# Attention scores laid out with keys on the partitions and kept in SBUF until the maximum is known

## The chip, the cores and the metric

One NeuronCore of a Trainium2 chip runs the whole kernel. The metric is device time in microseconds (us). Engines are named as in the profile: PE (TensorE matmuls), PEld (its weight loads), DVE (VectorE), ACT (ScalarE), POOL (GpSimd), SP (SyncE, which issues the DMAs). PE writes only PSUM; ACT and DVE read PSUM; POOL works on SBUF.

## The reference, cut to what matters

```
x: (8, 2048, 256) f32;  W_qkv: (256, 768)
xn = layernorm(x)
q, k, v = split(xn @ W_qkv)
scores = q @ k.T / 16, causal mask (keys after the query are -inf)
attn = softmax(scores) @ v
out = x + attn + ffn(xn)          # ffn: a shared expert and one of 32 routed experts for each token
```

## The kernel before

Four stages run one after the other: `token_stage` (layer norm, shared expert, router), `routing_stage`, `expert_stage` (the routed experts), and `attention_stage`, the last one, which the change rewrites. Everything before about 1443 us of the profile is untouched.

Matrix products are made in three float32r passes of split operands, hi*hi, lo*hi, hi*lo (`split_matmuls`, L69 to L71). The weights of q and k are folded into one 256x256 matrix, so "queries" are x times that matrix and the keys are x itself.

In `attention_stage` there are 8 batches of 16 row blocks of 128 queries (B = 8, NB = 16). For each batch PE makes the queries (8 units of 512 columns), the values (8 units), and then for each row block i: the scores of its 128 queries (on partitions) against all (i+1)*128 keys, in up to four PSUM banks, with a bf16 matmul that adds the causal mask (L1243). DVE reduces them to the row maximum (L1101), ACT takes the exponential with its row sum (L1168), PE turns each 128x128 block so that keys come on partitions (L1255), ACT writes the high part of the turned block (L1177), DVE the low part (L1109), and PE weighs the values with them (136 blocks of a batch, three matmuls of 256 columns each). DVE scales the row by 1/sum and adds `base` (L1120).

POOL prepares `base` of each row block: `sum1` = routed + shared row (L1074), `base` = sum1 + x (L1076), then it copies the positions of the row block after next (L1058) and issues their gather (L1060). The program order on each engine is written out by hand. PE makes the scores of row i+1 between the transposes and the weighing of row i, so that DVE and ACT have that time for the softmax.

## Time and profile before

| | |
|---|---|
| time, median of 3 runs | 2554.9 us (2553.63, 2554.90, 2556.84) |
| span of the profiled execution, first to last instruction | 2553.1 us |
| busy: PE, PEld, DVE, ACT, POOL | 98%, 90%, 61%, 43%, 30% |
| attention stage in the profile | from 1443 us to the end |

A busy share is the time in which at least one instruction of the engine is under way. PE's matmuls overlap, so the cost of one in a dense stream is the distance from its start to the next start, which the timeline shows, and not its duration. The profile does not give the profiled execution's time apart from its span; the span is 0.5 us below the fastest of the three runs and 1.8 us below their median.

### The profile page before, as it was taken

How to read it: one execution, taken by the hardware profiler on the slowest of the kernel's cores; microseconds unless marked ns; L12 is line 12 of the kernel's file. 1: busy time of each engine (PE TensorE's matmuls, PEld its weight loads, DVE VectorE, ACT ScalarE, POOL GpSimd, SP SyncE). 2: the span in 40 equal slices, each digit the busy share in tenths (PEclk: the TensorE clock that was granted, in tenths of full speed). 3: DMA queues.
4: the chain of work that ended last, by engine and by line, in shares of the span. 5: the costliest groups of instructions: out<-in, count | busy, mean ns of one | idle time of the engine just before them, and what ended most of it. 6: DMA issues, size and time to landing. Idle time of an engine off the chain costs nothing. (4 is left out here: it accounts for less than half of the span.)

```text
span 2553.1 us, 51599 instructions
## 1 busy us (share of the span) xinstructions
PE 2491.2 (98%) x17497; PEld 2296.7 (90%) x17497; DVE 1565.0 (61%) x3433; ACT 1095.4 (43%) x1901; POOL 758.7 (30%) x920
## 2 busy tenths in 40 slices
PE   7999999998879999999999799999999999999999
PEld 5888888887779999999999799999999999999998
DVE  7777777775967777777777444544444444444453
ACT  3333333333646655566555333333333333333332
POOL 1111111110034444444444342423232322323141
PEclk9999999999889999999999899999999999999999
DMA  4434434342367777777777732322323232323230
GB/s 141 149 128 139 143 133 141 136 139 101 135 224 237 237 231 238 236 240 236 233 234 239 226 110 71 116 82 84 113 67 120 73 114 63 110 79 110 67 94 19
DMA packets 264190, 369.37 MB, mean 145 GB/s; under 512 B 17424, under 2 KB 186896, under 8 KB 264080
## 3 DMA queue, kind: packets, MB, share of 16 engines
q1 hardware_dynamic: 250064, 329.60, 38.3%
q0 software_dynamic: 14016, 38.29, 6.0%
q8 instruction: 71, 1.16, 0.2%
q14 instruction: 39, 0.32, 0.0%
HBM read 254.57 MB, written 113.25 MB: 144 GB/s over the span
## 5 line engine op out<-in xcount | busy, mean ns | idle before, releaser
L69 PE MATMUL t_psO<-t_v_hi,t_pT_hi 128*128 128x256 f32 x1088 | 316.1, 291 | 0.5 <-DVE t_pT_lo L1109 0.5
L71 PE MATMUL t_psO<-t_v_lo,t_pT_hi 128*128 128x256 f32 x1088 | 307.5, 283 | 0.0
L70 PE MATMUL t_psO<-t_v_hi,t_pT_lo 128*128 128x256 f32 x1088 | 307.2, 282 | 0.0
L1101 DVE TENSOR_REDUCE t_negmax<-t_psS 128x1 f32<-128x128 f32 (+15 forms) x128 | 165.1, 1290 | 217.0 <-PE t_psS L1243 216.7
L1168 ACT ACTIVATE t_prob<-t_psS,t_negmax 128x128 f32<-128x128 f32 (+15 forms) x128 | 149.9, 1171 | 337.0 <-DVE t_negmax L1101 335.8
L832 DVE TENSOR_TENSOR e_wlo<-e_raw,e_whi 128x1024 fp32r<-128x1024 f32 x162 | 198.1, 1223 | 152.2 <-ACT e_whi L875 152.2
L1074 POOL TENSOR_TENSOR t_sum<-t_routed,t_shr 128x256 f32<-128x256 f32 x128 | 94.2, 736 | 639.6 <-DVE t_outb L1120 624.9
L808 POOL DMA_INDIRECT e_xg<-xs_rows,e_slot x164 | 248.5, 1515 | 97.0 <-POOL e_slot L804 63.2
L1177 ACT CAST t_pT_hi<-t_psT 128x512 fp32r<-128x512 f32 (+2 forms) x320 | 152.0, 530 | 281.2 <-PE t_psT L1255 281.2
L69 PE MATMUL t_psS<-t_x_hi,t_q_hi 128*128 128x512 f32 (+2 forms) x640 | 243.4, 380 | 0.0
L71 PE MATMUL t_psS<-t_x_lo,t_q_hi 128*128 128x512 f32 (+2 forms) x640 | 233.0, 364 | 0.0
L70 PE MATMUL t_psS<-t_x_hi,t_q_lo 128*128 128x512 f32 (+2 forms) x640 | 232.4, 363 | 0.0
L1109 DVE TENSOR_TENSOR t_pT_lo<-t_psT,t_pT_hi 128x512 fp32r<-128x512 f32 (+2 forms) x320 | 180.3, 606 | 63.4 <-ACT t_pT_hi L1177 63.1
L69 PEld LDWEIGHTS t_psO<-t_v_hi,t_pT_hi 128*128 128x128 f32 x1088 | 208.5, 192 | 1.1 <-DVE t_pT_lo L1109 0.8
L70 PEld LDWEIGHTS t_psO<-t_v_hi,t_pT_lo 128*128 128x128 f32 x1088 | 208.1, 191 | 0.3
L71 PEld LDWEIGHTS t_psO<-t_v_lo,t_pT_hi 128*128 128x128 f32 x1088 | 207.9, 191 | 0.0
L69 PE MATMUL e_psD<-e_whi,e_h_hi 128*128 128x256 f32 x640 | 187.1, 292 | 4.3 <-issue 4.3
L69 PE MATMUL e_psG<-e_x_hi,e_whi 128*128 128x256 f32 x640 | 180.0, 281 | 3.6 <-DVE e_x_lo L840 3.6
L70 PE MATMUL e_psD<-e_whi,e_h_lo 128*128 128x256 f32 x640 | 180.7, 282 | 0.0
L71 PE MATMUL e_psD<-e_wlo,e_h_hi 128*128 128x256 f32 x640 | 180.3, 282 | 0.0
L71 PE MATMUL e_psU<-e_x_lo,e_whi 128*128 128x256 f32 x640 | 180.0, 281 | 0.0
L69 PE MATMUL e_psU<-e_x_hi,e_whi 128*128 128x256 f32 x640 | 179.7, 281 | 0.0
(190 smaller groups left out, 7287.2 us busy)
## 6 DMA issues: line engine op xcount, KB each, us to landing
e_raw<-in_L_ffn_routed_gate_w SPq DMA_DIRECT2D x83, 512.0 KB
e_raw<-in_L_ffn_routed_up_w SPq DMA_DIRECT2D x83, 512.0 KB
e_raw<-in_L_ffn_routed_down_w SPq DMA_DIRECT2D x82, 512.0 KB
routed_rows<-e_dout SPq DMA_DIRECT2D x80, 256.0 KB
a_xt<-in_L_attn_x SPq DMA_DIRECT2D x32, 512.0 KB, 4.5
xT_high<-a_xT_hi SPq DMA_DIRECT2D x32, 512.0 KB, 3.7
xT_low<-a_xT_lo SPq DMA_DIRECT2D x32, 512.0 KB, 3.9
xs_rows<-a_xs SPq DMA_DIRECT2D x32, 512.0 KB, 3.0
```

Source lines behind the costliest of these rows:

```text
L69: nc.tensor.matmul(out, hi, rhi, start=first, stop=False, skip_group_check=True)
L70: nc.tensor.matmul(out, lo, rhi, start=False, stop=False, skip_group_check=True)
L71: return nc.tensor.matmul(out, hi, rlo, start=False, stop=last, skip_group_check=True)
L808: g.indirect_dma_start(out=xg[:, k, h], out_offset=None, in_=xs, in_offset=bass.IndirectOffsetOnAxis(slot[:, k, h:h + 1], 0)).then_inc(x_i ...
L832: v.tensor_tensor(wlo[k][:, n], raw[k][:, n], whi[k][:, n].bitcast(F32), ALU.subtract).then_inc(wlo_ok, 1)
L1074: g.tensor_tensor(sum1[:, k], routed[:, k], shr[:, kg, j], ALU.add).then_inc(sum_ok, 1)
L1101: v.tensor_reduce(negmax[:, i % 2:i % 2 + 1], psS[:].rearrange("p a n -> p (a n)")[:, 0:(i + 1) * P], AX.X, ALU.max, negate=True).then_inc ...
L1109: v.tensor_tensor(pT_lo[s][:, 0:m], psT[:, (before[i] + q) % 3, 0:m], pT_hi[s][:, 0:m].bitcast(F32), ALU.subtract).then_inc(pl_ok, 1)
L1168: s.activation(prob[i % 2][:, 0:(i + 1) * P], psS[:].rearrange("p a n -> p (a n)")[:, 0:(i + 1) * P], ACT.Exp, bias=negmax[:, i % 2:i % 2 ...
L1177: s.copy(pT_hi[t][:, 0:m], psT[:, (before[i] + q) % 3, 0:m]).then_inc(ph_ok, 1)
```

## The change

Only `attention_stage` changes. Scores come with 128 keys on the partitions and up to 512 queries (a group of four row blocks) in the free dimension, so nothing has to be turned before the values are weighed. A tile (b, G, j) is key block j for query group G: 4(G+1) tiles in a group, the last four on the diagonal and cut to 512, 384, 256, 128 columns; 40 tiles in a batch, 320 in all. The order of a batch is G = 0, 1, 2, 3, with 4, 8, 12, 16 tiles.

Because the maximum of a query is now over partitions and over tiles, ACT copies each score tile to SBUF (`keep_score`, a ring of 21 slots) and DVE folds it into a running maximum over tiles (`highest`). After a group, PE turns this [128, 512] tile (`turn`, four transposes), DVE reduces it and spreads it on a diagonal (`row_max`), one matmul with ones brings it to all partitions (`broadcast`), and ACT stores it (`keep_shift`). POOL adds this shift to every stored score tile, in place (`lower`). ACT then takes the exponential twice, once as f32 and once rounded as the high part (`exps`), DVE makes the low part (`p_low`), and PE weighs the values 21 steps after the scores (`weigh`), into four PSUM banks, one for each row block of the group; a column of ones beside the values gives the row sum.

All engines walk through one list of steps; a step is one score tile, and engines differ in how many steps they lag. POOL's work on the rows (`sum1`, `base`, `gather`) is the same as before; it now shares the queue with `lower`. Score PSUM is three banks.

The diff, cut to its core (the old lines are those of the listing above; PE's `queries`, `values` and the loads change in indices only):

```diff
+class Plan:
+    LAG = 21
+    BANKS = 3
...
+        self.tiles = [(b, G, j) for b in range(B) for G in range(GB) for j in range(J * (G + 1))]
...
+            q_step.setdefault(max(0, self.first[g] - 3), []).append(g)
+                v_step.setdefault(self.first[g] + 10 + u, []).append((g, u))
...
+    XR, VR, QR, PR, HR = 5, 5, 2, 3, 3
+    W = D + 2
+    plan = Plan(B, NB, GB)
+    LAG, BANKS, T = plan.LAG, plan.BANKS, plan.T
+    SR = LAG
...
+            def load_rows(n):
+                k, g, h = n % 2, n // 2, n % 2
+                wait(sp, base_ok, 2 * (n - 1))
+                sp.dma_start(xr[:, k], x_g[g][:, 2 * h:2 * h + 2]).then_inc(r_in[k], 16)
+                sp.dma_start(shr[:, k], sh_g[g][:, 2 * h:2 * h + 2]).then_inc(r_in[k], 16)
...
+            def gather(r):
+                k = r % 2
                 wait(pool, sum_ok, r - 1)
+                wait_apart(pool, d_in[k], 16 * (r // 2), passed)
+                g_.tensor_copy(pos[:, k], keep.position[:, r:r + 1]).then_inc(pos_ok, 1)
                 wait_apart(pool, pos_ok, r + 1, passed)
+                g_.indirect_dma_start(out=routed[:, k], out_offset=None, in_=d_rows,
+                                      in_offset=bass.IndirectOffsetOnAxis(pos[:, k, 0:1], 0)).then_inc(d_in[k], 16)
+            def add_up(r):
+                k, n = r % 2, r // 2
+                wait(pool, r_in[n % 2], 32 * (n // 2 + 1))
+                wait(pool, d_in[k], 16 * (r // 2 + 1))
+                g_.tensor_tensor(sum1[:, k], routed[:, k], shr[:, n % 2, r % 2], ALU.add).then_inc(sum_ok, 1)
+                wait(pool, sum_ok, r + 1)
+                wait(pool, o_ok, r - 1)
+                g_.tensor_tensor(base[:, k], sum1[:, k], xr[:, n % 2, r % 2], ALU.add).then_inc(base_ok, 1)
+                if r + 2 < R:
+                    gather(r + 2)
+            def lower(t):
+                g, c0 = plan.group(t), plan.cut(t) * P
+                wait(pool, shift_ok, g + 1)
+                wait(pool, u_act, plan.s_unit[t] + 1)
+                s = score[:, t % SR, c0:]
+                g_.tensor_tensor(s, s, shift[:, g % HR, c0:], ALU.add).then_inc(sub_ok, 1)
+            g_.memset(ones[:].bitcast(F32), 1.0).then_inc(ones_ok, 1)
+            g_.memset(v_hi[:, :, :, D:D + 1].bitcast(F32), 1.0).then_inc(ones_ok, 1)
+            g_.memset(v_hi[:, :, :, D + 1:W].bitcast(F32), 0.0).then_inc(ones_ok, 1)
+            gather(0)
+            gather(1)
+            for step in range(T + LAG + 2):
+                t = step - LAG + 4
+                if 0 <= t < T:
+                    lower(t)
+                if 0 <= step - LAG + 2 < T:
+                    for r, _ in plan.rows_done(step - LAG + 2):
+                        add_up(r)
...
+            def highest(t):
+                g, c0 = plan.group(t), plan.cut(t) * P
+                _, G, j = plan.tiles[t]
+                m, s = top[:, g % 2, c0:], score[:, t % SR, c0:]
+                if j == 0 and G > 0:
+                    return
+                wait(dve, u_act, plan.s_unit[t] + 1)
+                if j < 2:
+                    wait(dve, top_mm, g - 1)
+                if G == 0 and j == 0:
+                    v.tensor_copy(m, s).then_inc(top_ok, 1)
+                elif G > 0 and j == 1:
+                    v.tensor_tensor(m, score[:, (t - 1) % SR, c0:], s, ALU.max).then_inc(top_ok, 1)
+                else:
+                    wait(dve, top_ok, plan.tops[t - 1])
+                    v.tensor_tensor(m, m, s, ALU.max).then_inc(top_ok, 1)
+            def row_max(g):
+                wait(dve, top_mm, g + 1)
+                v.tensor_reduce(negmax[:], psX[:].rearrange("p (a n) -> p a n", a=J), AX.X, ALU.max,
+                                negate=True).then_inc(max_ok, 1)
+                wait(dve, max_ok, g + 1)
+                wait(dve, shift_mm, g)
+                v.tensor_tensor(spread[:], keep.ident[:].unsqueeze(1).to_broadcast([P, J, P]),
+                                negmax[:].unsqueeze(2).to_broadcast([P, J, P]), ALU.mult).then_inc(spread_ok, 1)
+            def p_low(t):
+                c0 = plan.cut(t) * P
+                wait(dve, exp_ok, t + 1)
+                wait(dve, pv_mm, t - PR + 1)
+                v.tensor_tensor(p_lo[:, t % PR, c0:], prob[:, t % 2, c0:], p_hi[:, t % PR, c0:].bitcast(F32),
+                                ALU.subtract).then_inc(lo_ok, 1)
+            def output(t, r, a):
+                k = r % 2
+                wait(dve, pv_mm, t + 1)
+                v.reciprocal(rinv[:, k:k + 1], psO[:, a, D:D + 1]).then_inc(rinv_ok, 1)
                 wait(dve, rinv_ok, r + 1)
                 wait(dve, base_ok, r + 1)
+                wait(dve, o_out[k], 16 * (r // 2))
+                v.scalar_tensor_tensor(out=outb[:, k], in0=psO[:, a, 0:D], scalar=rinv[:, k:k + 1], in1=base[:, k],
                                        op0=ALU.mult, op1=ALU.add).then_inc(o_ok, 1)
+            for step in range(T + LAG + 2):
+                for g in plan.q_step.get(step, ()):
+                    for c in range(C):
+                        q_low(g, c)
+                if step < T:
+                    for g, u in plan.v_step.get(step, ()):
+                        v_low(g, u)
+                    highest(step)
+                for g in plan.ended_at(step - 1):
+                    row_max(g)
+                if 0 <= step - LAG + 1 < T:
+                    p_low(step - LAG + 1)
+                if 0 <= step - LAG - 1 < T:
+                    for r, a in plan.rows_done(step - LAG - 1):
+                        output(step - LAG - 1, r, a)
...
+            def keep_score(t):
+                n, c0 = plan.s_unit[t], plan.cut(t) * P
+                wait(act, exp_ok, t - SR + 1)
+                wait(act, u_mm, n + 1)
+                s.copy(score[:, t % SR, c0:], psS[:, n % BANKS, c0:]).then_inc(u_act, 1)
+            def keep_shift(g):
+                if g >= HR:
+                    wait(act, sub_ok, plan.last[g - HR] + 1)
+                wait(act, shift_mm, g + 1)
+                s.copy(shift[:, g % HR], psX[:]).then_inc(shift_ok, 1)
+            def exps(t):
+                c0 = plan.cut(t) * P
+                wait(act, sub_ok, t + 1)
+                wait(act, lo_ok, t - 1)
+                s.activation(prob[:, t % 2, c0:], score[:, t % SR, c0:], ACT.Exp)
+                wait(act, pv_mm, t - PR + 1)
+                s.activation(p_hi[:, t % PR, c0:], score[:, t % SR, c0:], ACT.Exp).then_inc(exp_ok, 1)
+            for step in range(T + LAG + 2):
+                for g in plan.q_step.get(step, ()):
+                    for c in range(C):
+                        q_high(g, c)
+                if step < T:
+                    for g, u in plan.v_step.get(step, ()):
+                        v_high(g, u)
+                    keep_score(step)
+                for g in plan.ended_at(step - 2):
+                    keep_shift(g)
+                if 0 <= step - LAG + 2 < T:
+                    exps(step - LAG + 2)
...
+            def free_bank(n):
+                if n - BANKS in plan.splits:
+                    wait(pe, split_ok, plan.splits[n - BANKS])
+                else:
+                    wait(pe, u_act, n - BANKS + 1)
...
+            def scores(t):
+                n, g, c0 = plan.s_unit[t], plan.group(t), plan.cut(t) * P
+                b, G, j = plan.tiles[t]
+                k, q = (b * GB + j // J) % XR, g % QR
+                diagonal = j >= J * G
+                cols = slice((j % J) * P, (j % J + 1) * P)
+                wait(pe, split_ok, plan.splits[plan.q_unit[g, C - 1]])
+                free_bank(n)
+                for d in range(C):
+                    mm = split_matmuls(nc, psS[:, n % BANKS, c0:], x_hi[:, k, d, cols], x_lo[:, k, d, cols],
+                                       q_hi[:, q, d, c0:], q_lo[:, q, d, c0:], d == 0, d == C - 1 and not diagonal)
+                if diagonal:
+                    mm = nc.tensor.matmul(psS[:, n % BANKS, c0:c0 + P], keep.mask_bf[:], keep.ident_bf[:],
+                                          start=False, stop=True, skip_group_check=True)
+                mm.then_inc(u_mm, 1)
+            def turn(g):
+                wait(pe, top_ok, plan.tops[plan.last[g]])
+                wait(pe, shift_ok, g)
+                for a in range(J):
+                    mm = nc.tensor.transpose(psX[:, a * P:(a + 1) * P], top[:, g % 2, a * P:(a + 1) * P], keep.ident[:])
+                mm.then_inc(top_mm, 1)
+            def broadcast(g):
+                if g == 0:
+                    pe.wait_ge(ones_ok, 3)
+                wait(pe, spread_ok, g + 1)
+                nc.tensor.matmul(psX[:], ones[:], spread[:].rearrange("p a n -> p (a n)"),
+                                 start=True, stop=True).then_inc(shift_mm, 1)
+            def weigh(t):
+                b, G, j = plan.tiles[t]
+                g, kv, kp = b * GB + G, (b * GB + j // J) % VR, t % PR
+                wait(pe, split_ok, plan.splits[plan.v_unit[b * GB + j // J, (j % J) // 2]])
+                wait(pe, lo_ok, t + 1)
+                for a in range(plan.cut(t), J):
+                    cols = slice(a * P, (a + 1) * P)
+                    last = j == J * G + a
+                    if j == 0:
+                        wait(pe, o_ok, (g - 1) * J + a + 1)
+                    nc.tensor.matmul(psO[:, a, 0:W], p_hi[:, kp, cols], v_hi[:, kv, j % J], start=j == 0, stop=False,
+                                     skip_group_check=True)
+                    nc.tensor.matmul(psO[:, a, 0:W], p_lo[:, kp, cols], v_hi[:, kv, j % J], start=False, stop=False,
+                                     skip_group_check=True)
+                    mm = nc.tensor.matmul(psO[:, a, 0:D], p_hi[:, kp, cols], v_lo[:, kv, j % J, 0:D], start=False, stop=last,
+                                          skip_group_check=True)
                 mm.then_inc(pv_mm, 1)
+            for step in range(T + LAG):
+                for g in plan.q_step.get(step, ()):
+                    for c in range(C):
+                        queries(g, c)
+                if step < T:
+                    for g, u in plan.v_step.get(step, ()):
+                        values(g, u)
+                    scores(step)
+                for g in plan.ended_at(step - 1):
+                    turn(g)
+                for g in plan.ended_at(step - 2):
+                    broadcast(g)
+                if 0 <= step - LAG < T:
+                    weigh(step - LAG)
```

## Rows read from the trace of the kernel before

**Rows 1.** The page, busy time of each engine over the span.
```profile
PE 2491.2 (98%) x17497; PEld 2296.7 (90%) x17497; DVE 1565.0 (61%) x3433; ACT 1095.4 (43%) x1901; POOL 758.7 (30%) x920
```
**Rows 2.** Busy time by stretch: PE, PEld, DVE, ACT, POOL, clock, DMA.
```profile
1718.00:1855.00 137.00, 137.00 (x944) 125.47 (x943) 62.47 (x104) 47.93 (x88) 41.54 (x64) 1.00 0.29 93
1855.00:1992.00 137.00, 137.00 (x944) 125.51 (x944) 62.48 (x104) 47.95 (x88) 41.55 (x64) 1.00 0.29 93
```
**Rows 3.** The chain that ended last, from 1440 us to the end, by line.
```profile
by line: PE t_psS L69 17.5%; PE t_psS L71 17.0%; PE t_psS L70 17.0%; PE t_psO L69 12.0%; PE t_psO L71 11.6%; PE t_psO L70 11.6%; PE t_psT L1255 10.9%; PE t_psS L1243 0.8%; DMA t_x_lo<-xT_low 0.5%; issue 0.3%; ACT L1168 0.1%; DVE t_pT_lo L11
```
**Rows 4.** Timeline of PE (start, duration, instruction).
```profile
2300.55 0.60 PE L1255 MATMUL t_psT<-keep_ident,t_prob 128*128 128x128 f32 x4
2300.91 0.48 PE L69 MATMUL t_psS<-t_x_hi,t_q_hi 128*128 128x512 f32 x1
2301.22 0.39 PE L70 MATMUL t_psS<-t_x_hi,t_q_lo 128*128 128x512 f32 x1
...
2302.38 0.28 PE L69 MATMUL t_psS<-t_x_hi,t_q_hi 128*128 128x256 f32 x1
...
2303.09 0.23 PE L1243 MATMUL t_psS<-keep_mask_bf,keep_ident_bf 128*128 128x128 bf16 x1
2303.12 0.37 PE L69 MATMUL t_psS<-keep_v_hi,t_x_hi 128*128 128x256 f32 x1
2303.33 0.28 PE L70 MATMUL t_psS<-keep_v_hi,t_x_lo 128*128 128x256 f32 x1
...
2306.07 0.71 PE L1255 MATMUL t_psT<-keep_ident,t_prob 128*128 128x128 f32 x5
2306.53 0.47 PE L69 MATMUL t_psS<-t_x_hi,t_q_hi 128*128 128x512 f32 x1
```
**Rows 5.** Groups by shape, ACT and DVE, from 1480 us (busy, mean ns).
```profile
L1177 ACT CAST t_pT_hi<-t_psT 128x512 fp32r<-128x512 f32 x223 | 120.2, 593 | 127.8 <-PE t_psT L1255 127.8
L1109 DVE TENSOR_TENSOR t_pT_lo<-t_psT,t_pT_hi 128x512 fp32r<-128x512 f32 x223 | 143.7, 687 | 62.9 <-ACT t_pT_hi L1177 62.9
L1120 DVE SCALAR_TENSOR_TENSOR t_outb<-t_psO,t_rinv,t_base 128x256 f32<-128x256 f32 x125 | 60.5, 484 | 162.8 <-issue 159.4 <-DVE t_rinv L1115 1.5
L1115 DVE RECIPROCAL t_rinv<-t_rowsum 128x1 f32<-128x1 f32 x125 | 19.2, 154 | 0.0
```
**Rows 6.** Timeline of POOL in the attention stage, one row block.
```profile
2301.76 0.74 POOL L1074 TENSOR_TENSOR t_sum<-t_routed,t_shr 128x256 f32<-128x256 f32 x1 [0.22 <-DVE t_outb L1120]
2302.58 0.74 POOL L1076 TENSOR_TENSOR t_base<-t_sum,t_xr 128x256 f32<-128x256 f32 x1
2303.27 0.18 POOL L1058 COPY t_pos<-keep_position 128x1 int32<-128x1 int32 x1
2304.27 0.99 POOL L1060 DMA_INDIRECT t_routed<-routed_rows,t_pos  x1 [0.82 <-POOL t_pos L1058]
```
**Rows 7.** Timeline of POOL and DVE in the routing stage, 638 to 650 us.
```profile
638.90 4.43 DVE L632 TENSOR_TENSOR r_moved<-ranks_one_hot,r_shift 128x4096 f32<-128x4096 f32 x1
...
640.30 4.15 POOL L583 TENSOR_TENSOR keep_v_lo<-r_wqkv,keep_v_hi 128x512 fp32r<-128x512 f32 x1 [3.73 <-ACT keep_v_hi L591]
...
647.83 1.39 POOL L585 TENSOR_TENSOR keep_a_lo<-r_a,keep_a_hi 128x512 fp32r<-128x512 f32 x1 [3.38 <-ACT keep_a_hi L597]
...
648.14 1.17 DVE L635 CAST r_pos_i<-r_pos 128x128 int32<-128x128 f32 x1
...
649.91 0.22 DVE L640 CAST r_token<-r_token_i 128x128 f32<-128x128 int32 x1
```
**Rows 8.** Timeline of POOL and DVE in the expert stage, 1199 to 1207 us.
```profile
1201.63 1.23 DVE L832 TENSOR_TENSOR e_wlo<-e_raw,e_whi 128x1024 fp32r<-128x1024 f32 x1 [2.01 <-ACT e_whi L875]
...
1201.95 1.76 POOL L808 DMA_INDIRECT e_xg<-xs_rows,e_slot  x1 [0.81 <-POOL e_slot L804]
...
1205.16 0.96 POOL L808 DMA_INDIRECT e_xg<-xs_rows,e_slot  x1 [1.45 <-issue]
```
**Rows 9.** Busy time by stretch in the routing stage (columns as in rows 2).
```profile
640.00:650.00 10.00, 5.36 (x16) 3.71 (x14) 9.83 (x8) 2.45 (x4) 5.54 (x2) 0.67 1.03 354
```

More of the change, by code:

```diff
@@ L960, in attention_stage @@
     J = GT // P
-    QU = C * GB
-    VU = NB // 2
-    groups = [i // 4 + 1 for i in range(NB)]
-    before = [sum(groups[:i]) for i in range(NB + 1)]
-    TG = before[NB]
-    assert TG % 4 == 0 and NB % 2 == 0 and C * GB % 4 == 0
+    XR, VR, QR, PR, HR = 5, 5, 2, 3, 3
[3 more added lines that the diff above has]
+    SR = LAG
+    NGR, R = plan.NGR, B * NB
     with ExitStack() as st:
@@ new lines, in store @@
+            def store(r):
+                wait(sp, o_ok, r + 1)
+                sp.dma_start(out_g[r // J][:, r % J], outb[:, r % 2]).then_inc(o_out[r % 2], 16)
+            for g in range(XR):
+                load_x(g)
+                if g < 2:
+                    load_rows(g)
+            for step in range(T + LAG + 2):
+                for g in range(XR, NGR):
+                    if plan.first[g] - 12 == step:
+                        load_x(g)
+                if 0 <= step - LAG - 1 < T:
+                    for r, _ in plan.rows_done(step - LAG - 1):
+                        store(r)
+                        if r % 2 == 1 and r // 2 + 2 < R // 2:
+                            load_rows(r // 2 + 2)
@@ L1116, in output @@
                 wait(dve, rinv_ok, r + 1)
-                wait(dve, pv_mm, b * TG + before[i + 1])
                 wait(dve, base_ok, r + 1)
-                wait(dve, o_out[k], 16 * half)
-                v.scalar_tensor_tensor(out=outb[:, k], in0=psO[:, k], scalar=rinv[:, k:k + 1], in1=base[:, k],
+                wait(dve, o_out[k], 16 * (r // 2))
+                v.scalar_tensor_tensor(out=outb[:, k], in0=psO[:, a, 0:D], scalar=rinv[:, k:k + 1], in1=base[:, k],
                                        op0=ALU.mult, op1=ALU.add).then_inc(o_ok, 1)
-            for u in range(QU):
-                q_low(0, u)
@@ L1201, in _, with q_high, v_high @@
-            each_pair(act, B // 2, pair)
+            def q_high(g, c):
+                n = plan.q_unit[g, c]
+                wait(act, u_mm, n + 1)
+                if g >= QR:
+                    wait(act, u_mm, plan.s_unit[plan.last[g - QR]] + 1)
+                s.copy(q_hi[:, g % QR, c], psS[:, n % BANKS]).then_inc(u_act, 1)
+            def v_high(g, u):
+                n = plan.v_unit[g, u]
+                wait(act, u_mm, n + 1)
+                if g >= VR:
+                    wait(act, pv_mm, plan.last_pv(g - VR) + 1)
+                s.copy(v_hi[:, g % VR, 2 * u:2 * u + 2, 0:D],
+                       psS[:, n % BANKS].rearrange("p (a d) -> p a d", a=2)).then_inc(u_act, 1)
@@ L1247, in transposes @@
-            def transposes(b, i, q):
-                n = b * TG + before[i] + q
-                s = (before[i] + q) % 3
-                if q == 0:
-                    wait(pe, exp_ok, b * NB + i + 1)
-                if before[i] + q >= 3:
-                    wait(pe, pl_ok, n - 2)
-                for m in range(4 * q, min(4 * q + 4, i + 1)):
-                    mm = nc.tensor.transpose(psT[:, s, m % 4], prob[i % 2][:, m * P:(m + 1) * P], keep.ident[:])
-                mm.then_inc(t_mm, 1)
```

345 lines of the change are left out of this document (108 added, 237 removed).

## The prediction

> **What bounds the kernel now.** I read the page first, then the busy time by stretch, the chain that ended last, the timelines, and the groups by shape. PE is busy 98% of the span [rows 1]. In the attention stage each batch takes 137.3 us with PE busy all of it, at full clock, and DVE, ACT and POOL less than half [rows 2]. The chain there is PE's from end to end: scores, queries and values 51%, weighing 35%, transposes 10.9% [rows 3]. So work taken off PE there shortens the time one for one, until another engine can't follow.
>
> **PE's prices** are start distances [rows 4]. A 512-column pass costs 0.232 us, from 2301.22 to 2302.38 for five; a 256-column pass 0.118, from 2302.38 to 2303.09 for six. Four transposes take 0.36 before the next matmul and lengthen that one by 0.08 (2300.91 to 2301.22 instead of 0.232): 0.09 each and 0.08 for each run of them. A mask matmul costs 0.12 in the same way.
>
> **What leaves PE, for a batch.** 136 transposes in 40 runs: 136*0.09 + 40*0.08 = 15.4 us, near the chain's 10.9% of 137. Score passes: off the diagonal both kernels have 24 pieces of 512 columns. On it the old kernel has widths 256, 256, 384, 512 in each group, the new one 512, 384, 256, 128: 24 passes go from 256 to 128 columns. No float32r pass of 128 columns is in this trace. Its floor is a transpose's 0.09, its ceiling a 512-column pass; I take the floor, gain 24*0.03 = 0.7, and keep 24*0.14 = 3.4 us loss as the other end. Queries, values, mask and weighing stay in count (408 passes of 256 columns; two more columns are 1/128 of that). **What comes:** four runs of four transposes, 1.8, and four 512-column passes, 1.0. Net 15.4 + 0.7 - 2.8 = 13.3 us saved, 124.0 of PE work in a batch, 107 us in the stage.
>
> **What ACT and DVE get.** ACT: a 512-column copy is 0.59 [rows 5], and a tile needs three such passes, 1.8 us, where a step of PE is on average 124/40 = 3.1. DVE: two 512-column operations a tile at 0.69 [rows 5], 1.4 us, and the four maxima, low parts and outputs. Neither is a bound by itself. POOL is.
>
> **POOL's new load.** A row block costs 0.82 (sum to base) + 0.69 (base to copy) + 1.00 (copy to gather) + 0.99 (gather), 3.5 us, 3.7 with what lies before the next operation [rows 6]. `lower` is a two-input operation of 512 columns, which takes 1.39 us when nothing is in its way [rows 7], with its handoff 1.5; the cut tiles at 2.9 ns a column (0.74 for 256 [rows 6]) 1.15, 0.8 and 0.45. A batch is 24*1.5 + 4*3.9 + 16*3.7 = 111 us, against PE's 124: 41.5 before [rows 2], when it waited for the rest.
>
> **Where it can't hide.** Each diagonal tile carries a row block, and the four diagonal tiles of G = 3 are followed at once by the four of the next batch's G = 0: eight in a row. A cycle of POOL there is 3.7 + a lower, 4.2 to 5.2 us. It can't be done ahead: `base` of row r waits for `output` of r-2, which DVE makes only after the next score tile is made and copied (1.4 + 0.6), `highest` and `p_low` (0.7 each) and its own 0.15 + 0.48 [rows 5], with handoffs 4.3 us behind the weighing. Behind that `base` in POOL's queue stand the gather and the `lower` of the tile three further on; for that wait ACT's exponentials, behind them ACT's next `keep_score`, which frees PE's banks, and DVE's `p_low`, for which PE's `weigh` waits.
>
> Number the tiles from the first diagonal one of G = 3 as 0, and set the clock to zero at its output, 4.3 us after its weighing. PE's next ten steps are, by its prices: ten score tiles 12.5 us (those 21 further on), two query units 2.8, two value units 2.8, `turn` and `broadcast` 0.8, weighings 10.0, together 28.8: alone it would end tile 10 at 24.5. On POOL the first wait is of tile 2's `base`, at zero; `lower` of tile 10 ends after 4.85 + 4.5 + 4.15 + 5.2 + 5.2 + 4.4 = 28.3. Two exponentials and a low part with handoffs (2.6 to 3) and 1.4 of weighing end tile 10 at 32.7: PE stands still 8 us. From there POOL has four lowers (5.0), a sum and three more cycles (15.3) to the `base` of tile 15, the last row of G = 1, at 48.7. Its output, some 2.3 later, is what the fourth block of tile 16 waits for, since that block overwrites its PSUM bank: 51.4 where PE would be at 47.4, 4 us more. After G = 2's four, `lower` of G = 3's first tile needs a shift that is ready only then (at S); two rows are queued behind it, and the second output comes at S + 4.8, so `lower` two tiles on ends at S + 14.4, its weighing at S + 18.5, where PE alone has S + 14.7: 4 us. 16 us a batch.
>
> **The lock.** A POOL operation that reads two operands ran 4.15 us instead of 1.39 for the same shape [rows 7]. It began at 640.30 while DVE worked on two SBUF inputs until 643.33, and ended 1.1 us after that. The other way round, a DVE cast of 128 columns, 0.22 elsewhere, took 1.17 us and ended with POOL's operation of 647.83 to 649.22. A gather took 1.76 us under such a DVE operation and 0.96 without [rows 8]. So one excludes the other for its whole length. In the old stage DVE's large operations have an operand in PSUM, and POOL's adds are a steady 0.74. In the new one `highest`, `p_low` and the spreading read two SBUF operands, and so does POOL. In a batch they hold the inputs about 50 us (77 tile operations of 0.29 to 0.69, four spreads) beside POOL's 75. In a cycle of the cluster DVE has 1.2 us of it. About 0.7 falls on POOL's adds and lowers, not on its 2 us around the gather, and a gather met by it loses 0.2: I take 0.9 a cycle (ends: 0, and all 1.2 with a wait on both sides, 1.8). The first cluster has five cycles before `lower` of tile 10 and a low part that is held too: its stall goes from 8 to 13.5. The second has four lowers and three cycles more, and waits for a `p_low` ahead of its output: 4 to 10.5. The third has two cycles: 4 to 6. 30 us a batch.
>
> The Trainium skill, "SBUF — State Buffer", section "Who interferes with whom", has this as a rule: a DVE instruction with two SBUF inputs contends with a GpSimd instruction that reads SBUF, and the later one blocks fully. By that rule, and the trace agrees, the sum is the one below; without it, it would be that of the second rival.
>
> **The sum.** Seven boundaries between batches at 24, the first batch's G = 0 and 1 at 12, eight third clusters at 6, and the end, where PE has no score tiles left to make between the weighings while POOL needs 50 us for 16 tiles and six rows: 20 more. 168 + 12 + 48 + 20 = 248, less 107: +141. 2553.1 + 141 = 2694 in the profiled execution, and with the 1.8 us to the median 2696. SP moves the same bytes beside a DMA share of 0.29 [rows 2]; its row loads now wait for every second output, 5 us ahead of their use, and cost nothing while POOL is late anyhow. The chain `turn`, `row_max`, `broadcast` (DVE 0.69 + 0.69 between two PE steps) holds PE where both steps are short, twice a batch by some 0.6 us; that falls into the same waits, and I count none of it.
>
> **Rivals.**
> POOL and the lock bound the stage, my forecast: 2696, own range 2630 to 2780 by the two ends of the lock and the narrow pass. Chance 0.50.
> The lock costs almost nothing, because DVE's operations fall beside the gather; the row cycles alone: 7*12 + 6 + 8*4 + 15 = 137, less 107, +30: 2585, between 2565 and 2630. For it: DVE is free half the time. Against it: 125 us of exclusive use in a batch where PE has 124 us of work. Chance 0.14.
> The other side, faster: POOL's row work doesn't hold `weigh`. Then PE waits only at each group's start, where its fourth block needs `output` of the row before, about 2 us, 64 us in the stage, with 10 at the end: 107 - 74 = 33, 2522. It decides at one point: a row cycle of POOL of at most 3.2 us, where `lower` of tile 10 comes at 20.4 instead of 28.3. For it: the 21 steps of distance. Against: 3.5 us are in the rows before any `lower`. Chance 0.18.
> Worse: PE, standing still again and again, gets its low clock. At 640 us, with PE busy half of a stretch, the granted clock was 0.67, between its two levels of 2.4 and 1.2 GHz [rows 9]. Half speed in the some 35 us of work of the clusters costs another 15 to 25 us a batch where it isn't hidden by POOL: 2820 to 2900. Chance 0.18.
>
> **The numbers.** A measurement of this kernel can tell some 0.2% from no change. The range goes from 2565 to 2880: it takes the first two and most of the last, and leaves out the faster case and the far end. Faster 0.17, same 0.03, slower 0.80.
>
> **What would show it.** In the profile after: L1255 gone but for 128 transposes; PE busy about 80% of the attention stage; a batch at 150 to 158 us; POOL over 80% busy there and first in the chain; idle time of PE before `weigh` put down to `p_low` or to `output`; `lower` of 512 columns with a minimum near 1.4 us and a mean of 1.8 to 2.1, DVE's `p_low` with the same scatter. I am wrong if `lower` is never longer than 1.5 us, if POOL waits for most of its time, or if PE's idle time lies at the groups' starts alone.

## The result and the profile after

| | before | after |
|---|---|---|
| median of 4 runs | 2554.98 us | 2780.18 us (2779.45 to 2783.1) |
| ratio | | 1.0882, 95% interval 1.0865 to 1.0898 |
| profiled span | 2553.1 us | 2781.3 us |

The change makes the kernel 8.8% slower: on the side that was forecast, 84 us above its point of 2696, inside the whole range (2565 to 2880), and just above the 2630 to 2780 that the forecast case had for itself. The page of the changed kernel, busy time of each engine:

```profile
PE 2493.6 (90%) x16569; PEld 2260.6 (81%) x16569; DVE 1872.3 (67%) x3665; ACT 1269.1 (46%) x2317; POOL 1197.2 (43%) x1243
```

PE was 98% busy [rows 1] and is 90% busy. Its busy sum has hardly moved although transposes are gone: at the low clock a pass takes nearly twice as long. The busy time by stretch says so (columns as in [rows 2]):

```profile
1600.00:1760.00 160.00, 133.73 (x815) 117.86 (x814) 99.84 (x133) 67.40 (x136) 92.47 (x101) 0.91 0.23 73
2240.00:2400.00 160.00, 129.46 (x798) 114.40 (x797) 96.65 (x129) 67.26 (x137) 93.74 (x104) 0.91 0.25 80
```

A batch takes about 165 us where it took 137 [rows 2]. PE stands for about 30 of them and has a mean granted clock of 0.91, where it had 1.00. POOL is busy for only 58% of them. The groups of POOL and DVE by shape (busy, mean ns, idle before):

```profile
L1145 POOL TENSOR_TENSOR t_score<-t_score,t_shift 128x512 f32<-128x512 f32 x224 | 282.7, 1286 | 149.1 <-ACT t_shift L1264 147.5
L1136 POOL TENSOR_TENSOR t_base<-t_sum,t_xr 128x256 f32<-128x256 f32 x128 | 117.4, 917 | 308.2 <-DVE t_outb L1216 300.2
...
L1191 DVE TENSOR_TENSOR t_top<-t_top,t_score 128x512 f32<-128x512 f32 x168 | 268.8, 1600 | 237.5 <-ACT t_score L1258 237.3
```

`lower` takes 1.29 us, less than the 1.39 of [rows 7], so POOL isn't held by DVE in it. Its other operations do pay something: `sum1` takes 0.97 us in the mean where it took 0.74, `base` 0.92 for 0.74, the copy of positions 0.40 for 0.18, the gather 1.03 for 0.99, together 0.67 us a row. The large change is on the other side. It is DVE's `highest` that has a mean of 1.60 us where two-input operations of that width took 0.69 [rows 5]. The two DVE lines one by one (least, median, largest duration in ns):

```profile
L1191 DVE TENSOR_TENSOR t_top<-t_top,t_score x264: 279/693/12762, 1459.6 to 2725.8; 128x512 f32<-128x512 f32 x84, 128x384 f32<-128x384 f32 x16, 128x128 f32<-128x128 f32 x16, 128x256 f32<-128x256 f32 x16
L1206 DVE TENSOR_TENSOR t_p_lo<-t_prob,t_p_hi x320: 276/684/13177, 1496.4 to 2775.6; 128x512 fp32r<-128x512 f32 x128, 128x256 fp32r<-128x256 f32 x32
```

The median is undisturbed, the largest is 12.8 and 13.2 us: 17 operations of 512 columns last over 3 us, 145 us together. The timeline of POOL, of DVE and of PE around one of them:

```profile
2251.70 0.99 POOL L1126 DMA_INDIRECT t_routed<-routed_rows,t_pos  x1 [0.81 <-POOL t_pos L1124]
2252.72 15.64 POOL L1145 TENSOR_TENSOR t_score<-t_score,t_shift 128x512 f32<-128x512 f32 x13
2268.32 1.17 POOL L1133 TENSOR_TENSOR t_sum<-t_routed,t_shr 128x256 f32<-128x256 f32 x1
```
```profile
2255.71 12.08 DVE L1191 TENSOR_TENSOR t_top<-t_top,t_score 128x512 f32<-128x512 f32 x1 [3.65 <-ACT t_score L1258]
2267.70 1.21 DVE L1206 TENSOR_TENSOR t_p_lo<-t_prob,t_p_hi 128x512 fp32r<-128x512 f32 x1
```
```profile
2256.53 0.39 PE L71 MATMUL t_psS<-t_q_lo,t_x_hi 128*128 128x512 f32 x1
2269.06 0.55 PE L1355 MATMUL t_psO<-t_v_hi,t_p_hi 128*128 128x258 f32 x1 [12.14 <-DVE t_p_lo L1206]
2269.41 0.42 PE L1357 MATMUL t_psO<-t_v_hi,t_p_lo 128*128 128x258 f32 x1
2269.62 0.41 PE L1359 MATMUL t_psO<-t_v_lo,t_p_hi 128*128 128x256 f32 x1
```

POOL makes a gather and then 13 shifts without a gap, 1.20 us each. DVE begins one `highest` in the middle of that run and ends it 12.08 us later, 0.5 us before the run does. `p_low` is behind it in DVE's queue, PE's weighing waits for that, and when PE goes on its passes stand 0.21 us apart instead of 0.118 [rows 4]: the low clock. This happens once a batch, in G = 3's run. A smaller one, 4 to 7 us, comes in G = 2's shorter run.

**Where the time went.** From PE's records in the attention stage I took the time between one's end and the next one's start, and the stretches with a granted clock under 0.75. In those PE was busy 177 of 262 us; I counted half of the 177 as lost, and the rest as work at full clock. The passes' own distances give a little less: 0.214 us for 0.118, and 0.427 for 0.232, are a loss of 45%, some 80 us instead of 89. The split is good to some 10 us in another way too: *noshift*, *gap* and *early* (below) make the same matmuls and read 1016, 1028 and 1028 us of work.

| us in the stage | before | after | predicted for after |
|---|---|---|---|
| work at full clock | 1099 | 1014 (-85) | -107 |
| PE idle | 1 | 227 | +248 |
| lost to the low clock | 1 | 89 | none in the sum; a rival |
| the stage | 1101 | 1330 | |

The idle time ahead of the weighings, by the tile weighed, sorts into the prediction's clusters (us a batch): the first (G = 0 and 1) 7.8, the second (G = 2) 5.7, the third (G = 3) 13.7. The prediction had 13.5, 10.5 and 6. The sum is about right and its places are not. By single tiles, 93 of the 227 us stand ahead of tile 26 (the third of G = 3), the one that the long `highest` holds up. Another 66 stand ahead of the fourth block of the groups' first tiles (0, 4, 12, 24 of a batch), where PE waits for `output`. Ahead of tile 6, the prediction's tile 10, it is 0.6 us a batch, where the prediction had the 8 us of its first cluster. PE at those places in one batch (tile 0's fourth block, tile 4's fourth block, tile 6's first):

```profile
2323.15 0.39 PE L1355 MATMUL t_psO<-t_v_hi,t_p_hi 128*128 128x258 f32 x1 [2.86 <-DVE t_outb L1216]
...
2339.09 0.58 PE L1355 MATMUL t_psO<-t_v_hi,t_p_hi 128*128 128x258 f32 x1 [3.80 <-DVE t_outb L1216]
...
2346.56 0.28 PE L1355 MATMUL t_psO<-t_v_hi,t_p_hi 128*128 128x258 f32 x1
```

### The profile page after: what moved, and what is told of

Read it like the earlier page. It is cut to its first block and busy times, and to the rows that moved or that the text cites. A ratio compares the mean times of both kernels' runs of the same rounds, so it can differ in the third digit from the quotient of the medians.

```text
span 2781.3 us, 52329 instructions
## 1 busy us (share of the span) xinstructions
PE 2493.6 (90%) x16569; PEld 2260.6 (81%) x16569; DVE 1872.3 (67%) x3665; ACT 1269.1 (46%) x2317; POOL 1197.2 (43%) x1243
## 5 line engine op out<-in xcount | busy, mean ns | idle before, releaser
L1355 PE MATMUL t_psO<-t_v_hi,t_p_hi 128*128 128x258 f32 x1088 | 344.9, 317 | 217.1 <-DVE t_p_lo L1206 125.1
L1191 DVE TENSOR_TENSOR t_top<-t_top,t_score 128x512 f32<-128x512 f32 (+3 forms) x264 | 317.6, 1203 | 275.0 <-ACT t_score L1258 274.6
L1355 PEld LDWEIGHTS t_psO<-t_v_hi,t_p_hi 128*128 128x128 f32 x1088 | 222.7, 205 | 252.6 <-issue 174.0
L1145 POOL TENSOR_TENSOR t_score<-t_score,t_shift 128x512 f32<-128x512 f32 (+1 forms) x320 | 358.0, 1140 | 150.1 <-ACT t_shift L1264 147.5
L1357 PE MATMUL t_psO<-t_v_hi,t_p_lo 128*128 128x258 f32 x1088 | 322.8, 297 | 0.0
L1359 PE MATMUL t_psO<-t_v_lo,t_p_hi 128*128 128x256 f32 x1088 | 321.7, 296 | 0.0
L1206 DVE TENSOR_TENSOR t_p_lo<-t_prob,t_p_hi 128x512 fp32r<-128x512 f32 (+1 forms) x320 | 289.0, 904 | 17.5 <-ACT t_p_hi L1272 17.4
L69 PE MATMUL t_psS<-t_q_hi,t_x_hi 128*128 128x512 f32 (+3 forms) x640 | 246.7, 385 | 1.4 <-DVE t_q_lo L1167 1.4
L70 PE MATMUL t_psS<-t_q_hi,t_x_lo 128*128 128x512 f32 (+3 forms) x640 | 245.6, 384 | 0.0
L71 PE MATMUL t_psS<-t_q_lo,t_x_hi 128*128 128x512 f32 (+3 forms) x640 | 244.3, 382 | 0.0
```

The costliest lines, as they stand in the source:

```text
L69: nc.tensor.matmul(out, hi, rhi, start=first, stop=False, skip_group_check=True)
L70: nc.tensor.matmul(out, lo, rhi, start=False, stop=False, skip_group_check=True)
L71: return nc.tensor.matmul(out, hi, rlo, start=False, stop=last, skip_group_check=True)
L1145: g_.tensor_tensor(s, s, shift[:, g % HR, c0:], ALU.add).then_inc(sub_ok, 1)
L1191: v.tensor_tensor(m, m, s, ALU.max).then_inc(top_ok, 1)
L1206: v.tensor_tensor(p_lo[:, t % PR, c0:], prob[:, t % 2, c0:], p_hi[:, t % PR, c0:].bitcast(F32), ALU.subtract).then_inc(lo_ok, 1)
```

## The experiments

All ratios are to the kernel before in the same session (medians 2555.3 to 2556.3 us), with their 95% interval. Theory A: POOL's shifts follow each other so closely that a DVE operation with two SBUF inputs is shut out of a whole run of them. Theory B, the prediction's: the row cycle of POOL with a small toll for each contact. Theory C: DVE's in-order queue is the bound.

**gap.** `lower` waits until the shift before it is finished:

```
+                wait(pool, sub_ok, t)
                 s = score[:, t % SR, c0:]
```

> Each of POOL's shifts (lower) waits until the one before it has finished, which leaves a gap of under 0.1 us between two of them. Theory A (a run of POOL's shifts without a gap keeps a DVE operation with two SBUF inputs out until the whole run is over): DVE's longest highest or p_low falls from 13 us to under 2.5 us, PE's idle time before weigh put down to p_low falls from 125 us to under 50, and the time falls by 60 to 110 us, to 2670 to 2720 us. Theory B (the loss is POOL's row cycle in the runs of diagonal tiles, as in the prediction): the gap costs POOL 320 times 0.08 us, the time stays within 2770 to 2800 us.

Measured: 2676.71 us, ratio 1.0482 (1.0464 to 1.0499), 103 us faster than the changed kernel though a wait is added. The largest `highest`, in the view of that line:

```profile
L1192 DVE TENSOR_TENSOR t_top<-t_top,t_score x264: 281/696/2552, 1458.4 to 2623.0; 128x512 f32<-128x512 f32 x84, 128x384 f32<-128x384 f32 x16, 128x128 f32<-128x128 f32 x16, 128x256 f32<-128x256 f32 x16
```

12.8 us has become 2.6 (and `p_low`'s 13.2 has become 2.9); theory A had asked for less than 2.5. PE's wait for `p_low` has gone from 125 to 41 us. PE idles 139 us and loses 57 to the low clock. So theory A holds for 103 us. The clusters are now 6.8, 4.1 and 4.9 us a batch, near the 8, 4 and 4 that the prediction had before it added the lock, but not for its reason: 54 of the 139 us are waits for `output` at the groups' starts, and ahead of tile 6 there are still only 0.6 us a batch.

**noshift.** The shift is left out: POOL only counts, and the exponentials take the unshifted scores scaled by 0.001. The kernel then lacks the subtraction of the maximum, though it still finds, turns and spreads it.

```
-                g_.tensor_tensor(s, s, shift[:, g % HR, c0:], ALU.add).then_inc(sub_ok, 1)
+                pool.sem_inc(sub_ok, 1)
```

> Leaves the shift out of the computation: POOL only counts the semaphore on, and the exponentials take a scale of 0.001 so that their arguments stay small. POOL has the row work alone. Theory A: 2520 to 2570 us, PE waits mainly at the starts of the groups for output. Theory B: the cycle of 3.7 us a row still holds the runs of eight diagonal tiles, 3 to 6 us of standing a batch: 2560 to 2610 us.

Measured: 2553.08 us, ratio 0.9991 (0.9982 to 1.0001). PE's waits in the whole kernel, longest sums (us, times, longest):

```profile
PE t_psO L1354 <- DVE t_outb L1215: 40.7, 31, 2.9
PE t_psO L1354 <- issue: 17.9, 21, 1.4
```

Some 59 us at the groups' starts, where the faster rival had 64; 41 of them are the wait of the fourth block for `output`. The time is that of theory A (2520 to 2570). The work saved pays just for the idle time and the low clock (67 idle and 19 lost). So without the shift the two kernels are level, and the 225 us between them come with it.

**nogather, onegather, sync1.** What opens the run to DVE? In *nogather* all gathers but the first two are left out, with their copies of positions, so later rows take stale routed values. *onegather* keeps of them only the one of each group's last row. *sync1* is the changed kernel with one completion wait, at the second shift after each gather:

```
+                if plan.rows_done(t - 4) and t >= 4:
+                    wait(pool, sub_ok, t)
```

> Leaves out all gathers of routed rows but the first two, and their position copies; the two adds of a row stay. A row costs POOL 1.6 us instead of 3.7. Theory A: POOL runs further ahead and the long waits of DVE stay, the time falls only by the part of the row cycle: 2690 to 2750 us. Theory B: POOL keeps up with PE everywhere: 2540 to 2600 us.

> As the run without gathers (which leaves the routed rows out), but with the one gather of each group that stands right before the run of shifts off the diagonal. Theory A2: the long waits of DVE come back, with DVE operations of 5 to 13 us in the runs of G = 2 and 3, and the time rises from 2649 by 50 to 100 us, to 2700 to 2750 us, though POOL has only 2 us a group more to do. Theory A1 gives no reason for a change: 2645 to 2670 us, no DVE operation over 2 us.

> As the changed kernel, but the second shift after each gather waits until all before it have finished; within a run of 4 to 13 shifts no further wait stands. Theory A1 (any run of POOL operations without a gap keeps DVE out): one gap lets one DVE operation in, the rest of the run still keeps the next one out for 5 to 10 us; the time stays above 2730 us. Theory A2 (the gather leaves POOL's parts out of step, and only then does a run without a gap keep DVE out; one wait for completion brings them in step again, and from then on DVE gets its turn after each shift): DVE's longest operation falls under 3 us and the time is that of the run with a gap before every shift, 2660 to 2690 us.

| | us | ratio (interval) |
|---|---|---|
| nogather | 2649.43 | 1.0369 (1.0352 to 1.0386) |
| onegather | 2794.49 | 1.0934 (1.0915 to 1.0952) |
| sync1 | 2668.75 | 1.0444 (1.0426 to 1.0461) |

*nogather* came out under theory A's range and above B's, so both were wrong as they stood. Its longest DVE operation is 1.9 us, although POOL's runs have no gap in them:

```profile
2034.71 15.97 POOL L1143 TENSOR_TENSOR t_score<-t_score,t_shift 128x512 f32<-128x512 f32 x11
```
```profile
2041.91 1.68 DVE L1189 TENSOR_TENSOR t_top<-t_top,t_score 128x512 f32<-128x512 f32 x1 [4.34 <-ACT t_score L1256]
2043.51 1.77 DVE L1204 TENSOR_TENSOR t_p_lo<-t_prob,t_p_hi 128x512 fp32r<-128x512 f32 x1
```

So a run without a gap is not enough to shut DVE out. That is why A was split into A1 (any such run does it) and A2 (only one behind a gather does). *onegather* and *sync1* both speak for A2; *onegather* goes beyond its 2700 to 2750 us and its 13 us for one operation. *nogather* also bears on theory B: `lower` of the prediction's tile 10 ends 20.2 to 22.1 us behind the first output, near the 20.4 at which the prediction's faster rival was to come true with 2522 us. The time is 2649, and PE waits 70.6 us for `output`.

The timeline of *onegather*, POOL and DVE:

```profile
2093.63 0.99 POOL L1126 DMA_INDIRECT t_routed<-routed_rows,t_pos  x1 [0.81 <-ACT t_score L1258]
2094.64 15.07 POOL L1145 TENSOR_TENSOR t_score<-t_score,t_shift 128x512 f32<-128x512 f32 x13
```
```profile
2094.53 16.42 DVE L1206 TENSOR_TENSOR t_p_lo<-t_prob,t_p_hi 128x512 fp32r<-128x512 f32 x1
2110.87 0.15 DVE L1212 RECIPROCAL t_rinv<-t_psO 128x1 f32<-128x1 f32 x1
```

One gather ahead of the run, with its copy of positions, is enough: `p_low` takes 16.42 us. It began 0.11 us before the run did, while the gather was still under way, and still lost. And of *sync1* in the same kind of run:

```profile
2037.44 17.18 POOL L1147 TENSOR_TENSOR t_score<-t_score,t_shift 128x512 f32<-128x512 f32 x12 [0.17 <-POOL t_score L1147]
```
```profile
2040.04 1.71 DVE L1193 TENSOR_TENSOR t_top<-t_top,t_score 128x512 f32<-128x512 f32 x1 [4.34 <-ACT t_score L1260]
2041.67 1.77 DVE L1208 TENSOR_TENSOR t_p_lo<-t_prob,t_p_hi 128x512 fp32r<-128x512 f32 x1
2044.01 1.13 DVE L1193 TENSOR_TENSOR t_top<-t_top,t_score 128x512 f32<-128x512 f32 x1 [0.57 <-ACT t_score L1260]
```

After one wait of 0.17 us the engines take turns: POOL's shift goes from 1.20 to 1.43 us in the mean (17.18 for 12), DVE's operations take 1.1 to 1.8. The gather's own 1 us isn't the cost (*nogather* gains only 19 us over *sync1*). What it leaves behind is, and one completion wait clears it. No run parts the gather from the copy of positions just ahead of it.

**dve.** DVE makes all the shifts, at `step - LAG + 3`, between its `p_low` and `output`:

```
+                if 0 <= step - LAG + 3 < T:
+                    lower(step - LAG + 3)
```

> DVE makes the shift, one step ahead of the exponentials; POOL has the row work alone. DVE's load of a batch goes from 75 to about 100 us, under PE's 124. Theory A: no run of POOL is left, DVE's operations stay under 1.5 us: 2540 to 2620 us. Theory B: about the same from POOL, but a theory C, DVE's in-order queue becomes the bound with three operations of 0.69 us a tile behind each other, would give 2640 us or more.

Measured: 2659.60 us, 1.0414 (1.0396 to 1.0431). No `highest` or `p_low` lasts over 1.5 us (the longest shift is 1.7), as theory A asked, yet the time isn't A's 2540 to 2620, and only 17 us under *gap*. PE waits 91.7 us, 55 times, for `output`, which stands behind three operations of DVE's step, and 1.6 us for `p_low`. That is theory C: DVE's queue.

**early, rows.** *early* is *gap* with `output` moved from the end of DVE's step to its start. *rows* is *early* with the gather reading `keep.position` itself, without POOL's copy and the wait for it.

> The gap before every shift, and DVE's output moved from the end of its step to the start, before highest and p_low. The fourth block of each group's first tile waits for it: 54 us of PE's idle time in the run with the gap, 41 without any shift. I expect 20 to 50 us less than 2677: 2627 to 2657 us. If POOL's row cycle alone sets the time there, POOL gets its release earlier too, but no more than that.

> As the run before, and the gather takes its positions from the kept table itself, without the copy and the wait for it: POOL's row goes from 3.7 to about 2.0 to 2.5 us. If the row cycle in the runs of diagonal tiles carries most of the 124 us between the runs with and without the shift, the time falls by another 40 to 80 us, to 2560 to 2600 us; if the lock between POOL and DVE carries it, by less than 25 us.

*early* 2618.63 us, 1.0246 (1.0229 to 1.0263): 58 us off *gap*, more than the 20 to 50 expected. So the place of `output` in DVE's step was worth that much. PE's longest waits in it:

```profile
PE t_psO L1356 <- DVE t_p_lo L1207: 73.0, 73, 2.9
PE t_psO L1356 <- issue: 31.2, 22, 2.1
```

Its wait for `output`, 54.4 us in *gap*, has nearly gone (2.1), while the one for `p_low` has grown from 40.9. *rows* 2624.03 us, 1.0267 (1.025 to 1.0284), where 2560 to 2600 was expected if the row cycle carried most of what was left. POOL's row cycle did get shorter: `lower` of the prediction's tile 10 ends 24.4 to 26.2 us behind the first output, 27.8 to 31.4 in *early*. The time didn't fall. So the length of the row cycle is not what holds this kernel.

**warm.** The changed kernel with 75 matmuls of ones that nobody reads, where PE waits longest, to keep it busy:

```
+                if G == 3 and j == 2:
+                    wait(pe, shift_ok, min(g + 2, NGR))
+                    for _ in range(75):
+                        nc.tensor.matmul(psX[:, 0:P], ones[:], ones[:], start=True, stop=True)
```

> The changed kernel, with 75 extra matmuls of 128 columns (ones by ones, into a bank that is free then, read by nobody) that TensorE runs at tile 26 of each batch, just before it waits for that tile's p_low. At 0.11 us a pass they take about 8 us, and TensorE idles 11.6 us there a batch in the changed kernel (92.6 us over 8 batches), so they should lie inside the idle time. Theory (the idle time brings the clock down, and the passes that follow run at half speed: 89 us of the 2780 by my reading of the trace, most of it behind this wait): the granted clock stays up, the batches get 3 to 8 us shorter, 2715 to 2755 us. Rival (the low clock follows from something else, or its passes run inside later waits anyway): 2775 to 2790 us, with the granted clock up or not. A second rival, the extra matmuls come to lie on the path where the wait is short: over 2790.

Measured: 2782.57 us, 1.0882 (1.0864 to 1.09): no gain. PE's timeline in the same batch as above:

```profile
2257.73 8.49 PE L1352 MATMUL t_psX<-t_ones 128*128 128x128 f32 x75
...
2271.40 0.58 PE L1359 MATMUL t_psO<-t_v_hi,t_p_hi 128*128 128x258 f32 x1 [5.18 <-DVE t_p_lo L1206]
```

The matmuls lay inside the wait as meant, but PE idles 5.18 us more behind them, and its first pass then still takes 0.58. By my count the low clock costs 76 instead of 89 us, while waits at other tiles grew by 9. The little clock won was used up by waiting. The time is the first rival's. The run speaks against counting all 89 us as time that a full clock would give back, but it touched only 13 of them, and their true worth stays open.

**lag24, split24, behind24.** *lag24* is *early* with `LAG` 24 instead of 21. *split24* is *lag24* with the shifts of odd tiles on DVE, each engine counting in a semaphore of its own. *behind24* gives DVE only those tiles whose shift would stand right behind a row's sums on POOL:

```
+        behind = [t >= 3 and bool(plan.rows_done(t - 3)) for t in range(T)]
```

> The kernel 'early' (a completion wait ahead of every shift, output moved to the start of DVE's step; 2618.6 us) with the distance between a tile's scores and its weighing raised from 21 to 24 steps. The tiles whose rows run on POOL between shifts then have three more steps (some 8 us) between the shift's arrival for the last group of a batch and its use. Theory (what is left is the late shifts in the rows' clusters, a latency): TensorE's waits at tiles 26 and 4 fall, 2580 to 2605 us. Rival (what is left is contention that lengthens DVE's p_low at every tile, a throughput): no gain, 2612 to 2630 us.

> As lag24, with the shifts of odd tiles made by DVE (three steps' distance before the tile is weighed plus one more) and those of even tiles by POOL. POOL then has half the shifts between its row sums, DVE some 76 more of 0.5 to 0.7 us (about 6 us a batch more than lag24, DVE then near 75% busy). Theory (POOL's shifts in the clusters of row sums, and the lock that they take with DVE, make the time that is left): 2550 to 2590 us, near the kernel before. Rival (DVE's in-order queue becomes the bound, as when it made all the shifts: 2659.6 us): 2600 to 2640 us.

> As split24 (2559.5 us), but DVE makes just the 16 shifts of a batch that would stand right behind a row's sums on POOL (tiles 3 to 6, 11 to 14, 23 to 26, 39 and the next 0 to 2), and POOL the 24 others. In split24 the time that is left stands mostly ahead of tiles 4, 6, 12, 14 and 24, whose shifts POOL makes behind row sums (8.3, 8.5, 5.0, 11.5 and, for tile 4, 12.6 + 7.3 us of TensorE's idle 87). Theory (POOL's late shifts are what is left): those waits go, some 30 to 45 us off, 2515 to 2540 us, faster than both kernels. Rival (DVE now has four shifts together with its outputs and is the late one there): 2555 to 2590 us, with TensorE still waiting for p_low at the same tiles.

| | us | ratio (interval) | PE idle | lost to clock |
|---|---|---|---|---|
| early | 2618.63 | 1.0246 (1.0229 to 1.0263) | 114 | 28 |
| lag24 | 2597.11 | 1.0159 (1.0142 to 1.0175) | 102 | 21 |
| split24 | 2559.52 | 1.0013 (1.0004 to 1.0023) | 79 | 14 |
| behind24 | 2577.02 | 1.0097 (1.007 to 1.0123) | 79 | 17 |

Busy time of *split24* in one stretch:

```profile
1600.00:1760.00 160.00, 150.64 (x982) 133.84 (x982) 114.62 (x174) 82.86 (x164) 84.73 (x91) 1.00 0.26 81
```

PE at full clock and 94% busy. *lag24* and *split24* came out in the ranges of their theories. *lag24* is not clean evidence for its own: PE's idle time ahead of tile 26 fell from 20 to 3 us, but ahead of tile 4 it rose from 16 to 21. *split24* takes back 221 of the 225 us and is no faster than the kernel before. *behind24* was to be faster than both and is a miss; the rival's time came. Its PE waits 23.6 us for `p_low`, where *split24*'s waits 33.8, and 22.1 for `output` instead of 7.9: DVE is late with the outputs now, and the idle sum is the same. The steps along the way were 103 us (*gap*), 58 (*early*), 22 (*lag24*) and 38 (*split24*). *behind24*'s runs scatter from 2570 to 2592, for which I can name no cause. No version beat the kernel before.

## Why the prediction was right, and where it was not

**Held.** PE bound the kernel before, and the transposes' work did leave it. No run turned that into a shorter time: *noshift* has the saving and gives it back in waits and low clock. **The length of POOL's row cycle** was nearly right: `lower` of tile 10 was to end 28.3 us after the first output. The timeline of POOL in the changed kernel (first, middle and last rows of that cluster):

```profile
2312.68 0.73 POOL L1136 TENSOR_TENSOR t_base<-t_sum,t_xr 128x256 f32<-128x256 f32 x1 [33.52 <-DVE t_outb L1216]
...
2325.03 0.47 POOL L1145 TENSOR_TENSOR t_score<-t_score,t_shift 128x128 f32<-128x128 f32 x1
2325.45 0.73 POOL L1133 TENSOR_TENSOR t_sum<-t_routed,t_shr 128x256 f32<-128x256 f32 x1
...
2339.33 5.86 POOL L1145 TENSOR_TENSOR t_score<-t_score,t_shift 128x512 f32<-128x512 f32 x5
```

The first of the five is tile 10's; it ends 26.65 + 1.2 = 27.9 us after 2312.68, and 27.9 to 31.3 us in the seven batches. With the lock as predicted, 0.9 us in each of five cycles, it would have been 32.8. There is some luck in that: the row work did pay a toll of 0.67 us a row, and `lower` was cheaper than the 1.5 us counted for it.

**The first step that failed: from the row cycle to PE.** The prediction had PE stand still 8 us before tile 10's weighing, because `lower` ends so late. The cycle has the length that it gave, and PE doesn't wait there: 0.6 us a batch. In that batch it gets there 2.6 us later than predicted, having already waited for `output` at the fourth blocks of tiles 4 and 8 (tiles 0 and 4 of the batch; 2.86 and 3.80 us in PE's rows of the section on the result). These waits were in the prediction, at about 2 us each, but only in the faster rival; its own sum took just the one at tile 16. They are 66 us in the changed kernel, 54 in *gap* and 41 in *noshift*, and *early*, which only moves `output`, is 58 us faster. Two runs shorten the cycle itself. *rows* ends `lower` of tile 10 some 3 us sooner and gains nothing. *nogather* ends it at 20.2 to 22.1 us, where by the prediction's own test the faster rival should have come true, and is still 94 us slower than the kernel before. What the shift costs beyond the shut-out and `output`'s place, some 60 us, was won back by a longer lag and by sharing the shifts; which wait it is, no run isolates.

**The second step that failed: the lock.** The prediction saw that one engine excludes the other for a whole operation, and made it "0.9 a cycle" on POOL's side, added to the row cycle. The runs showed that DVE pays far more, and not for one operation of POOL's but for all that follow one another after a gather: 12 to 13 us in G = 3's run (16 in *onegather*), which has no row in it and in which the prediction saw no danger. Hence 13.7 us a batch in the third cluster, where it had 6. *gap* and *sync1* take this part out alone, for 103 and 111 us. The idle total, 227 us for 248, is right by luck: too much behind the row cycle, and too little for the shut-out and for `output`. The Trainium skill, "SBUF — State Buffer", section "Who interferes with whom", has the contention as an exclusive lock, and the trace agrees on who contends. It says that whoever issues first holds the shared pair of ports "for the whole instruction"; a DVE operation shut out of a run of 11 to 13 instructions goes beyond that.

**The low clock left out of the sum.** It was a rival with 15 to 25 us a batch "where it isn't hidden by POOL". By my count it is 80 to 89 us, 10 or 11 a batch, in one with the forecast case and not instead of it. Put in, it closes the sum: 2694, plus 22 for less work saved, minus 21 for less idle time, plus 89 is 2784, where the profiled execution has 2781. That is bookkeeping, since all three terms are read from the trace that they are to explain. It doesn't say what a full clock would have given back, and *warm* speaks against all of it.

**Work saved: 85 for 107.** The new pass of 128 columns costs 0.11 us (five of them in *noshift*, 2102.58 to 2103.14), not the floor of 0.09 that the prediction took: 24 times 0.02 us, 4 us in the stage. Some 9 us more lie in each block's first weighing pass, 0.136 us to the next in *noshift* where it was 0.128 in the kernel before, 1088 times. The rest is within what the count itself can be off.

**Wrong signs to look for.** POOL was to be over 80% busy in the stage and is at 58%; a batch was to take 150 to 158 us and takes 165; `lower`'s mean of 1.8 to 2.1 is 1.29. Its own sign of being wrong, a `lower` never longer than 1.5 us, was nearly met (the longest is 1.64). The direction was right, and so was the place where the cost comes from: the shift on POOL, without which the two kernels are level. How it costs was another thing, and the wide range took that in.

## What to carry to other kernels

A move of work to GpSimd costs more than its own busy time: count for each DVE operation with two SBUF inputs how long GpSimd's runs of two-input operations are, and break a run behind an indirect DMA with one completion wait (111 us here). Before an engine's cycle is charged to the one that bounds, check that this one isn't already late there for another reason, and test it by shortening the cycle (*rows*). When all lost time comes as idle time of the bounding engine, look for one long instruction (the largest duration beside the median) before many small ones. And where the engine that bounds will stand still in a new schedule, the low clock belongs in the sum, as a term of its own.

## What the runs showed of the hardware

- A DVE operation with two SBUF inputs that meets a gapless run of GpSimd operations with two SBUF inputs, behind an indirect DMA, lasts until the run's end: 12.08 us at 13 shifts, 16.42 in *onegather*, where it had started 0.11 us before the first of them. Without the gather (*nogather*), or after one completion wait (*sync1*), the same two engines take turns, DVE's 512-column operations at 1.1 to 1.8 us and GpSimd's shifts at 1.43 to 1.45. What the gather leaves behind that does this, no run shows.
- GpSimd's adds of two SBUF inputs, 128 by 512, stand 1.16 to 1.20 us apart in such a run (15.07 for 13 in *onegather*, 15.64 for 13 in the changed kernel), under the 1.39 of [rows 7].
- After 5.18 us idle behind 8.49 us of matmuls, PE's next pass took 0.58 us (*warm*); at full clock the first pass after an idle time takes mostly 0.36 to 0.39 (*noshift*).
- At the low clock passes of 256 columns stand 0.214 us apart and passes of 512 columns 0.427, for 0.118 and 0.232 at full clock, so 45% of PE's busy time at the low clock is lost.
